# Self attention with its batch ends moved into the next batch, its maxima at steps 2 to 6 and its masks on the diagonal blocks alone, and the cross attention's first part inside it

## What is computed

```
xn = rmsnorm(ln) * norm_w                     # self attention, 16 heads of 8, causal
q, k, v = xn @ Wq.T + bq, xn @ Wk.T + bk, xn @ Wv.T + bv
x = x + xn + softmax(q k / sqrt(8), causal) v @ Wo.T + bo

q = ln @ Wq + bq                              # cross attention, 16 heads of 8
k, v = split(ctx @ Wkv + bkv)                 # ctx: 8 x 1601 x 96
x = x + softmax(q k / sqrt(8)) v @ Wo + bo

x = x + ffn(ln)                               # rotary attention (16 heads of 64), then a
                                              # mixture of 31 experts (3 active) and a shared one
```

## Time and profile before

| | us |
|---|---|
| median of 3 runs | 1735.83 |
| the profiled execution | 1737.37 |
| its span | 1735.6 |

### The profile page before, as it was taken

One profiled execution on the slowest core, in us unless ns is written; L12 is line 12 of the kernel. 1 busy time (PEld: TensorE's weight loads), 2 busy tenths in 40 slices (PEclk: granted clock), 3 DMA queues, 4 the chain that ended last, 5 costly groups with the idle time before them and its releaser, 6 DMA issues. The chain is left out here.

```text
span 1735.6 us, 29544 instructions
## 1 busy us (share of the span) xinstructions
PE 1531.3 (88%) x10917; PEld 833.4 (48%) x10941; DVE 1122.9 (65%) x2533; ACT 917.8 (53%) x1996; POOL 556.7 (32%) x692
## 2 busy tenths in 40 slices
PE   1667676599999999999999999699999998899998
PEld 1344343244444444444444544466666766544444
DVE  4745443487878787878878784556666655365554
ACT  1323233066677767677767767255555555343343
POOL 4010101121120303030303000578887788143331
PEclk9988887599999999999999999899999999799999
DMA  4222310803232323323222320000000000000001
GB/s 104 70 56 46 66 37 14 148 16 100 49 100 49 100 49 95 54 73 55 60 63 48 101 34 2 11 1 2 1 1 1 1 1 1 4 20 20 23 20 34
DMA packets 76978, 75.04 MB, mean 43 GB/s; under 512 B 12196, under 2 KB 66340, under 8 KB 75940
## 3 DMA queue, kind: packets, MB, share of 16 engines
q1 hardware_dynamic: 76836, 73.16, 19.1%
HBM read 42.47 MB, written 30.16 MB: 42 GB/s over the span
## 5 line engine op out<-in xcount | busy, mean ns | idle before, releaser
L1140 DVE TENSOR_REDUCE b_chunk_max<-psum 128x1 f32<-128x400 f32 (+1 forms) x1024 | 540.4, 570 | 161.4 <-PE psum L1346 154.2
L1275 ACT ACTIVATE b_prob<-psum 128x512 f32<-128x512 f32 (+1 forms) x832 | 450.4, 594 | 181.7 <-PE psum L1385 176.7
L1346 PE MATMUL psum<-k_stack,q_stack 128*128 128x400 bf16 (+1 forms) x1024 | 286.2, 343 | 21.0 <-DMA k_stack<-b_k_scratch 16.8
L1355 PE MATMUL psum<-b_prob,b_v_aug 128*32 128x256 f32 (+1 forms) x3328 | 265.8, 391 | 1.7 <-ACT b_prob L1275 0.4
L1385 PE MATMUL psum<-q_stack,k_stack 128*128 128x256 bf16 (+1 forms) x1664 | 253.8, 274 | 3.7 <-ACT b_prob L1275 3.3
L1385 PEld LDWEIGHTS psum<-q_stack,k_stack 128*128 128x128 bf16 (+1 forms) x1664 | 145.4, 99 | 122.8 <-ACT b_prob L1275 75.0
L1544 POOL TENSOR_SCALAR c_prob<-c_prob,c_rec 128x128 f32<-128x128 f32 (+1 forms) x256 | 192.5, 770 | 8.9 <-POOL c_kT L1553 8.3
L1959 DVE TENSOR_TENSOR e_hg<-e_gl,e_gate 128x512 f32<-128x512 f32 x124 | 123.4, 1018 | 88.3 <-PE psum L2007 83.9
L1627 DVE SCALAR_TENSOR_TENSOR c_turned<-psum,c_bias,c_tab 128x256 f32<-128x256 f32 x256 | 106.1, 476 | 112.0 <-PE psum L1760 112.0
L1662 ACT ACTIVATE c_prob<-psum,c_mneg 128x128 f32<-128x128 f32 (+1 forms) x256 | 104.3, 419 | 136.3 <-DVE c_mneg L1604 136.3
L1346 PEld LDWEIGHTS psum<-k_stack,q_stack 128*128 128x128 bf16 x1024 | 99.6, 98 | 131.9 <-DVE b_chunk_max L1140 97.4
(11 more groups left out here) (216 smaller groups left out, 1982.6 us busy)
## 6 DMA issues: line engine op xcount, KB each, us to landing
k_stack<-b_k_scratch SPq DMA_DIRECT2D x32, 600.4 KB, 10.2
b_k_scratch<-b_kparts SPq DMA_DIRECT2D x7, 1200.8 KB, 4.4
b_k_scratch<-b_kparts SPq DMA_DIRECT2D x7, 800.5 KB, 6.1
b_ctxT<-in_ctx SPq DMA_DIRECT2D x8, 600.4 KB, 11.9
e_w<-in_L_ffn_re_w SPq DMA_DIRECT2D x62, 64.0 KB, 1.9
a_scratch<-a_parts SPq DMA_DIRECT2D x16, 192.0 KB, 2.2
k_stack<-a_scratch SPq DMA_DIRECT2D x16, 192.0 KB, 4.7
q_stack<-b_q_scratch SPq DMA_DIRECT2D x32, 96.0 KB, 2.3
```

Source lines behind the costliest of these rows:

```text
L1140: nc.vector.tensor_reduce(out=chunk_max[:, half, q, column4(hh), c:c + 1], in_=max_bank(v)[:, 0:w], axis=AX.X, op=ALU.max).then_inc(max_do ...
L1275: nc.scalar.activation(prob[0:k, buf, par * 2 * T:(par + 1) * 2 * T], st_bank(v, par)[0:k, :], ACT.Exp, scale=HD ** -0.5).then_inc(exp_don ...
L1346: nc.tensor.matmul(max_bank(T_.now("unit"))[:, 0:hi - lo], queries_of(qst, h, slice(q * P, q * P + P)), keys_of(kst, h, slice(lo, hi)), st ...
L1355: last = nc.tensor.matmul(pv[32 * hh:32 * hh + 32, :], v_aug[0:k, kt, g * GH + hh, :], prob[0:k, buf, c:c + T], start=(kt == 0), stop=(kt ...
```

## The change

1. **Batch ends.** pv of the last group, attnT and out of batch b - 1 run at steps 0, 1 and 2 of batch b. A ninth round (b = 8) holds only these for batch 7. A third buffer holds the residual; the second key stack is a tile of its own.
2. **Units.** The 12 units of maxima stand at steps 2 to 6 (2, 2, 3, 3, 2), none at steps 0, 1 and 7. Item m stands at step 6. SP issues `store_m` and then the stack loads after the batch's last scores.
3. **Masks.** The scores are issued first and the mask after them, on the 128 diagonal columns of each head alone.
4. **Rows of maxima cleared.** `load_stack` of a query stack also writes zeros into its two rows of maxima: two more DMAs for each call, here and in the cross attention.
5. **Cross attention's first part.** Keys, query, values, splits, bounces and stack loads of batch 0 and 20 of the 32 units of its first head group run in batches 6 and 7 and the ninth round.
6. **Rotary weights.** They come in order from the host, each stored twice (2 MB instead of 1 MB), with 4 DMAs at the head of the cross attention's `load_weights`. POOL orders nothing.

The core of the diff (SP is `block.sync`, DVE `block.vector`, PE `block.tensor`; the last piece is the cross attention's prologue):

```diff
-        ITEMS_AT = {0: "v", 2: "x", 3: "pv", 4: "qk", 5: "pv", 7: "pv"}
-        UNITS_AT = [range(n * UNITS // STEPS, (n + 1) * UNITS // STEPS) for n in range(STEPS)]
+        UNITS_AT = [range(lo, hi) for lo, hi in ((0, 0), (0, 0), (0, 2), (2, 4), (4, 7), (7, 10), (10, 12), (12, 12))]
+        def items_of(b, n):
+            late, more, further = b >= 1, b + 1 < B, b + 2 < B
+            items = {0: [("v", b + 1, more), ("pv", b - 1, late)], 1: [("attnT", b - 1, late)],
+                     2: [("out", b - 1, late), ("x", b + 2, further)], 3: [("pv", b, b < B)], 4: [("qk", b + 2, further)],
+                     5: [("pv", b, b < B)], 6: [("m", b + 1, more)], 7: [("pv", b, b < B)]}[n]
+            return [(kind, of) for kind, of, there in items if there] + early.ITEMS.get((b, n), [])
...
+class CrossEarly:
+    ITEMS = {(6, 1): [("ck", 0)], (6, 2): [("ck", 1)], (6, 3): [("ck", 2)], (6, 4): [("ck", 3)], (6, 5): [("cx", 0)],
+             (6, 6): [("cq", 0)], (7, 0): [("cv", 0)], (7, 1): [("cv", 1)], (7, 2): [("cv", 2)], (7, 4): [("cv", 3)]}
+    UNITS = {(7, 6): range(0, 4), (7, 7): range(4, 8), (8, 0): range(8, 12), (8, 1): range(12, 16), (8, 2): range(16, 20)}
...
+            def stack(b):
+                sp.wait_ge(bounced, 2 * BOUNCES * 16 * (b + 1))
+                if b >= 2:
+                    sp.wait_ge(st_full, STEPS * (b - 1))
...
         @block.sync
...
+            def attend(b):
+                if b + 2 < B:
+                    bounce(b + 2)
+                if b == B - 2:
+                    for c, (lo, hi) in enumerate(CHUNKS):
+                        sp.wait_ge(early.k_split, c + 1)
+                        bounce_parts(sp, early.k_scr[:, :, lo:hi], early.kparts[:, :, lo:hi], 1,
+                                     early.k_bounced if c == 3 else early.chunks_bounced)
+                    sp.wait_ge(early.q_split, 1)
+                    bounce_parts(sp, early.q_scr, early.qparts[:], 0, early.q_bounced)
+                if b + 1 < B:
+                    store_m(b + 1)
+                if b + 2 < B:
+                    stack(b + 2)
+                if b == B - 2:
...
+                    for half, done in ((0, early.half_stacked), (1, early.stacked)):
+                        for which, operand, scr in ((0, qsts[0], early.q_scr), (1, t["kst"], early.k_scr)):
+                            load_stack(sp, operand, scr, which, slice(4 * half, 4 * half + 4), done, t["zero_rows"][:])
...
         @block.vector
...
+            def attend(b):
+                for n in steps_of(b):
+                    if b + 2 < B:
+                        norm(b + 2, n)
+                    if b == B - 2:
+                        early_norm(n)
+                    if b + 1 < B:
+                        maxima(UNITS_AT[n])
+                    for kind, of in items_of(b, n):
...
+                    early_units(early.UNITS.get((b, n), ()))
...
         @block.tensor
...
+            def attend(b):
+                if b < B:
+                    pe.wait_ge(m_stacked, 4 * 16 * (b + 1))
+                for n in steps_of(b):
+                    units = UNITS_AT[n] if b + 1 < B else range(0)
+                    if b < B:
+                        scores_t(b, n)
+                    maxima(b + 1, units[:1])
+                    if n >= 1 and b < B:
+                        values(b, n - 1)
+                    if n == 0 and b >= 1:
+                        values(b - 1, STEPS - 1)
+                    maxima(b + 1, units[1:])
+                    for kind, of in items_of(b, n):
...
-                nc.tensor.matmul(bank, identb[:], t[mask][:].rearrange("p h k -> p (h k)"), start=True, stop=False)
...
+                    nc.tensor.matmul(bank.rearrange("p (h k) -> p h k", k=keys)[:, :, keys - P:keys], identb[:],
+                                     t["mask_qk"][:, 0:len(heads), :], start=False, stop=True).then_inc(max_full, 1)
...
+def load_stack(sp, stack, scratch, which, tiles, sem, zero_rows):
...
     for i in range(2):
         sp.dma_start(stack_rows(stack, which, i, 0, NP * HD, tiles)[:, :, 0:n], v[i, :, tiles]).then_inc(sem, 16)
+        if which == 0:
+            sp.dma_start(stack_rows(stack, 0, i, SHIFT_ROW, 2, tiles)[:, :, 0:n], rows).then_inc(sem, 16)
...
     def load_weights(self, sp):
+        for m, name in enumerate(("q", "k")):
+            sp.dma_start(self.w12[:, m].rearrange("p w n -> p (w n)"), a["L0_ffn_%s_w" % name]).then_inc(self.w_loaded, 16)
+            sp.dma_start(self.bias[:, m].rearrange("p w u -> p (w u)"), a["L0_ffn_%s_b" % name]).then_inc(self.w_loaded, 16)
         sp.dma_start(self.vw[:], a["L0_ffn_v_w"]).then_inc(self.w_loaded, 16)
...
         @block.tensor
...
             def prologue():
-                for it in PROLOGUE_ITEMS[:-1]:
-                    item(*it)
-                pe.wait_ge(half_stacked, 4 * 16)
-                for u in range(UNITS_B):
+                for u in range(early.N_UNITS, UNITS_B):
                     unit(0, u)
```

More of the change, by code:

```diff
@@ L56, in build @@
         cross = CrossLoads(a, sb, sem)
[L57 removed]
         tables.allocate_weights(sb, sem)
[L59 removed]
+        with ExitStack() as middle:
+            early = CrossEarly(nc, lambda name, shape, dt=F32: middle.enter_context(nc.sbuf_tensor(name, shape, dt)), sem)
+            self_attention(nc, a, t, psum, s, tables, cross, own, early)
+            cross_attention(nc, a, t, psum, s, cross, tables, early)
         t["an_cur"] = sb("an_cur", [P, QT, D])
@@ L348, in self_attention @@
+def self_attention(nc, a, t, psum, s, tables, cross, pre, early):
     ctx = ExitStack()
@@ new lines, in early_item @@
+            def early_item(kind, g):
+                T_.up("item")
+                pe.wait_ge(prep_free, T_.now("item", 1))
+                if kind == "ck":
+                    if g == 0:
+                        pe.wait_ge(cross.w_loaded, cross.N_W * 16)
+                        pe.wait_ge(cross.ctx_loaded, 16)
+                    lo, hi = CHUNKS[g]
+                    last = nc.tensor.matmul(prep[:, 0:hi - lo], cross.wkv[:, 0:D], cross.ctxT[:, lo:hi], start=True, stop=True)
+                elif kind == "cx":
+                    pe.wait_ge(early.xn_ready, 1)
+                    for q in range(QT):
+                        last = nc.tensor.transpose(prep[:, q * P:(q + 1) * P], s["xn"][:, q, :], ident[:])
+                elif kind == "cq":
+                    last = nc.tensor.matmul(prep[:, 0:T], cross.wq[:], early.xT[:], start=True, stop=True)
+                elif kind == "cv":
+                    for j, kt in enumerate(range(4 * g, min(4 * g + 4, KT))):
+                        k = tile_rows(kt)
+                        last = nc.tensor.matmul(prep[0:k, j * D:(j + 1) * D], cross.ctxT[:, kt * P:kt * P + k], cross.wkv[:, D:2 * D],
+                                                start=True, stop=True)
+                last.then_inc(prep_full, 1)
+                if kind == "cv" and g == 3:
+                    pe.wait_ge(prep_full, T_.now("item"))
+                    pe.sem_inc(early.ctx_used, 1)
@@ new lines, in early_units @@
+            def early_units(units):
+                for u in units:
+                    if u == 0:
+                        pe.wait_ge(early.half_stacked, STACK_LOADS * 16)
+                    wait(pe, early.max_done, u - 1)
+                    q, c, hh = u // (4 * GH), u // GH % 4, u % GH
+                    lo, hi = CHUNKS[c]
+                    nc.tensor.matmul(psum[:, 2 + u % 2, 0:hi - lo], queries_of(t["qst"], hh, slice(q * P, q * P + P)),
+                                     keys_of(t["kst"], hh, slice(lo, hi)), start=True, stop=True).then_inc(early.max_full, 1)
@@ L781 @@
+            program(begin, attend)
 class Tally:
```

557 lines of the change are left out of this document (281 added, 276 removed).

## The result

The changed kernel takes 1721.59 us (median of 12 runs, 1711.15 to 1733.45) against 1735.74 (12 runs, 1734.25 to 1740.42): a ratio of 0.9915, interval 0.9891 to 0.9940. It is faster by 14 us. The forecast was faster, with 1711.5 and a range of 1692 to 1729: the side and the range hold, the size of the gain does not (24 were forecast). The new kernel's runs also spread over 22 us where those of before spread over 6; the slowest had a mean granted clock of 0.945 and the fastest 0.958. The profiled execution took 1722.1 us, with a span of 1720.3, at 0.949.

What follows compares the result with a forecast made beforehand. PE bounds the cross loop; no single engine bounds self attention, and the prologue ends in a 12.5 us key stack wait. Terms -0.8 - 1.0 - 3.2 - 24.9 + 1 + 4.5 = -24.4 gave 1711.5 us on the median's footing, range 1692 to 1729.

Steps and rivals of the forecast that it cites:

- Start, -0.8: Setup before the first scores: two masks made instead of four, with half the elements, shorten POOL's work by 0.8 us.
- Batches 1 to 5, -3.2: Self attention: period 30.0 us at half clock, 28.0 at full, against 30.6; five batches -3.2, bounds -13 and +3.
- the first piece: Batch start to item x: key stack wait of 3.59 us replaced by an engine chain, 11.65 at half clock against 11.7.
- x to m: Middle of a batch, item x to item m: DVE becomes the chain, 12.85 us against 13.49, PE staying at full clock.
- Rival A: The overlap pays throughout, smaller gaps keeping PE at full clock: -40.3 in all, 1695.5 us; chance 20%.
- Rival C: PE stays at 1.2 GHz from item x to item m, +5.6 us per batch: slower than before, 1752.5 us; chance 4%.
- Removing unit 0's wait for the keys: Batch start: unit 0 moves to step 2, after the key stack lands, taking away PE's 3.59 us wait.
- Batches 6, 7 and the prologue, -24.9: Cross attention's first part overlapped with the last batches: 94.9 us becomes 70.0, bounds -30 and -15.
- Rotary weights, +1: Cross block's start: 3 MB of weights issued before store_m(0) delay the m rows, +1 us, bounds 0 and +9.
- Rival B: The gain is spent on the queue: weights +9, zero rows +7, nothing from the batches, 1726 us; chance 19%.
- Zero rows, +4.5: Cross loop: two more DMAs of 0.46 us ahead of the keys delay seven stack loads, +4.5 us, bounds 0 to +7.
- Wrong if the cross loop grows by over 8 us: One of the forecast's stated signs of failure, against its own +4.5 us for the cross loop.

Runs made afterwards that it cites:

- e3_wide_masks: The changed kernel with its self attention masks over all columns again, four masks made in the setup: 1733.32 us, ratio 0.9977.
- e10_units_even: The changed kernel with its units of maxima dealt from step 0 on again, item m staying at step 6: 1737.84 us, ratio 1.0008.
- e6_m_rows_first: The changed kernel with store_m(7) issued by SP before it waits for the cross query's split and bounce: 1717.35 us, ratio 0.9889.
- e4_fill: The changed kernel with 14 unused mask matmuls ahead of PE's wait for the m rows in each batch: 1716.07 us, ratio 0.9872.
- e9_zero_last: The changed kernel with the zero rows' DMAs issued behind the keys, same DMAs, bytes and semaphore: 1711.37 us, ratio 0.9862.

## Why the prediction was right, and where it was not

**Start, -0.8: measured -3.3.** Of this 1.64 is POOL's first instruction, at 10.64 instead of 12.28. With wide masks it is at 12.78 and the first scores are at 60.59; in the ten kernels that have narrow masks the scores come at 56.6 to 57.9. So the start's gain belongs to the masks' edit, and my term counted only POOL's mask instructions, which themselves went from 1.76 to 1.04. Why POOL begins earlier the trace does not say ("issue"): DVE's clears, which POOL waits for, end near 2 us in all of them.

**Batches 1 to 5, -3.2: measured +0.4.** My period was 11.65 + 12.85 + 5.5 at half clock in the first piece. The first piece was better (10.2 to 11.0) and the last too (5.2). The links that I wrote out for the first piece add to 10.7, neither to 11.65 nor to the 9.7 at full clock; the five pieces came at 10.6 on average, at a clock of 0.66 to 0.81. The step that failed is "x to m", where I took over the full clock of before: "the work there stays dense". It doesn't: the waits for DVE ahead of x (up to 2.54 us) and at step 5 (2.14) are new. The new order makes them, with more for DVE to do between those places; the narrow masks do not, by e3_wide_masks. The piece took 14.4 to 17.5 us in four of five batches. The full-clock sum, 28.0, was right: 28.1 a batch with the gaps filled, and 9.67 + 13.07 + 5.15 in batch 3 against 9.7 + 12.85 + 5.5. Rival A's bound for the batches, -13, is what the fills earned. Rival C named the mechanism, PE at 1.2 GHz in x to m, and put it at every batch; it struck in some batches and parts of them, which cost the gain and not more. The Trainium skill ("TensorE: Matmul & The Clock Gate", section "A second HAM failure mode: psum-queue depth-cycling") tells of a PE that idles for short times between groups of matmuls and swings between its two clocks. This trace agrees, with idle times of 2.54 and 2.14 us ahead of stretches at 0.50, though batches in which the clock held after such a time stand beside it. For the batch's start I had cited the Trainium skill's case of a loop that waits for a DMA, and I had not asked for this one in its middle.

**Removing unit 0's wait for the keys** was the right reading: put back, it costs 16 us (e10_units_even). In the forecast's sum this stood only as the 3.59 that the first piece lost, against which a chain of nearly the same length was set.

**Batches 6, 7 and the prologue, -24.9: measured -24.3.** Batch 6 was forecast at 35.4 and took 35.49; its reason, `store_m(7)` queued on SP behind the wait for the query's split, is confirmed by e6_m_rows_first. The parts came as forecast as well: m at 25.0 (25.5 forecast), query matmul to split 4.2 (4.1), the query's bounce 2.3 (1.46), the m rows 3.9 (4.3). Batch 7 with the ninth round and the block's end was forecast at 34.6 and took 35.2.

**Rotary weights, +1: measured +0.1.** The 3 MB went out at 311.34 and the two largest landed in 4.7 and 6.5 us. `store_m(0)` was issued at 319.53 and landed for PE at 323.96, where PE waited 0.2. Rival B's main piece, +9, did not come.

**Zero rows, +4.5 with a bound of +7: measured 11.3 in the loop.** The mechanism was right, the size was not. I priced each DMA at 0.46 (a key load's issue) and it takes 0.68; and I counted only the delay, not what the clock takes after a wait that has grown from 1.34 to 2.67. The run without them gives about half to each. "Wrong if the cross loop grows by over 8 us" came true.

**The rest, -2.2.** All kernels run here lie between 647.8 and 652.8 us in this stretch, without a pattern by edit; nothing was tested there.

In all: the sum was -24.4 and the profiled execution's is -15.3. The start gave 2.5 more, the rest 2.2; the loop took 9.0, batches 0 to 5 took 5.1 more. The median lies in the range, at a gain of 14 us where 24 were forecast, and that is in part luck, since errors of both signs met. What the forecast had right is the term of batches 6 and 7, which carried it.

## What to carry to other kernels

A small DMA put ahead of a large one on the same queue costs its issue time, and more once the longer wait lowers TensorE's clock: what is small and not urgent goes behind. When a new order lets TensorE run ahead of the engine that paces a stretch, the idle times that this opens can lower its clock and cost what the order gains; read the granted clock in steps of a few us before and after, and fill all such gaps or move work into them. One gap filled (e4_fill) only moved the loss to the next. Ask of each wait on an issuing engine what is queued behind it: one reordered wait made batch 6 shorter by 5 us.

## What the runs showed of the hardware

- A DMA that writes two partitions of zeros from a two-partition source holds SyncE 0.64 to 0.73 us (0.89 at its first), and the larger load of the queries beside it mostly 0.31 to 0.44. Its place, not its bytes, decided 10 us (e9_zero_last).
- TensorE's granted clock fell to its lower level after idle times of 2.54 and 2.14 us in one batch, while batch 4 of the same execution, idle for 0.77 and 2.14 us at the same places, kept 1.00 from x to m, and so did batches 3 and 4 of e3_wide_masks with 2.3 and 1.93. So one such idle time alone does not settle it; batches of equal PE work took 28.39 to 33.54 us.
- 30 matmuls without a use in each batch made five batches 13 us faster (153.6 to 140.5 in the profiled executions, the clock from 0.83 to 1.00).
